# Low parts of eight value products made later, from unrounded copies, in a two-layer graph kernel

## The reference

```
h = relu(layernorm(x))
q, k, v = h @ Wq + bq, h @ Wk + bk, h @ Wv + bv
adj[src, dst] = 1
a = q @ k.T / sqrt(512);  a = a * adj + (1 - adj) * (-1e6)
x = x + softmax(a) @ v

h = relu(layernorm(x))
h = agg(h @ W1 + b1)            # normalised sum over edges and self loops
h = relu(gamma * (h - mean) / sqrt(var + 1e-5) + beta)     # over nodes
x = x + agg(h @ W2 + b2)
```

## Time and profile before

| | before |
|---|---|
| median of 3 runs | 307.56 us |
| profiled execution | 307.52 us |
| its traced span | 305.7 us |
| TensorE busy | 294.6 us (96%) |
| VectorE busy | 207.3 us (68%) |
| ScalarE busy | 160.0 us (52%) |
| GpSimd busy | 58.3 us (19%) |

### The profile page before, as it was taken

The page is one execution under the profiler, slowest core; times in us unless marked ns, Lnnn a source line. Parts: engine busy times, 40 slices in busy tenths (PEclk is TensorE's granted clock), DMA queues, the critical chain, the costliest instruction groups (busy, mean ns, idle before and its releaser), DMA issues.

```text
span 305.7 us, 4839 instructions
## 1 busy us (share of the span) xinstructions
PE 294.6 (96%) x1339; PEld 227.2 (74%) x1345; DVE 207.3 (68%) x458; ACT 160.0 (52%) x266; POOL 58.3 (19%) x103
## 2 busy tenths in 40 slices
PE   7999889899998999999999999999999999999995
PEld 6777346466665888888888888887888888878884
DVE  3889999999978557865758575568344388276311
ACT  3999967989546646545444454357523044342000
POOL 5352344000000530032131420203010044100000
PEclk9999999999999999999999999999999999999999
DMA  7816040000500309444362625323102000000221
GB/s 261 306 31 179 1 140 0 1 0 2 207 0 3 69 3 233 82 96 81 93 142 47 140 51 104 64 41 69 34 20 51 0 3 0 0 2 0 110 99 69
DMA packets 42312, 21.67 MB, mean 71 GB/s; under 512 B 35760, under 2 KB 36016, under 8 KB 42288
## 3 DMA queue, kind: packets, MB, share of 16 engines
q1 hardware_dynamic: 41744, 20.33, 26.3%
q10 hardware_dynamic: 544, 1.05, 1.0%
HBM read 10.88 MB, written 2.10 MB: 42 GB/s over the span
## 4 chain that ended last, share of the span: by engine, by line
PE 83%; DVE 8%; issue 3%; ACT 2%; DVEq 2%; DMA 1%; ACTq 0%
PE ps L986 19%; PE ps L988 19%; PE ps L987 18%; PE ps L1239 10%; PE ps L1162 8%; PE ps L1052 8%; DVE src_oh L705 1%; DMA qk_raw<-L_gnn_Wk_in 1%; DVE WT L688 1%; DVE M L688 1%; DVEq L705 1%; DVE wB L673 1%; DVE dst_oh L707 1%; PE ps L1020 1%; ACT lead_oh L473 0%
## 5 line engine op out<-in xcount | busy, mean ns | idle before, releaser
L705 DVE TENSOR_SCALAR src_oh<-iota,ecol 128x512 f16 x135 | 40.1, 352 | 5.0 <-issue 3.0
L1052 PE MATMUL ps<-src_oh,dst_oh 128*128 x131 | 33.3, 382 | 4.3 <-DVE dst_oh L707 3.1
L1162 PE MATMUL ps<-cnt,qh 128*128 128x512 f32 x128 | 30.1, 391 | 0.3 <-ACT cnt L575 0.3
L1052 PEld LDWEIGHTS ps<-src_oh,dst_oh 128*128 x135 | 13.3, 103 | 22.2 <-issue 12.8
L1239 PE MATMUL ps<-qh,cnt 128*128 128x512 f32 x128 | 29.3, 390 | 0.0
L1162 PEld LDWEIGHTS ps<-cnt,qh 128*128 128x128 f32 x128 | 23.9, 188 | 5.6 <-DVE qh L865 0.7
L1239 PEld LDWEIGHTS ps<-qh,cnt 128*128 128x128 f32 x128 | 23.9, 188 | 5.3 <-DVE vb L967 0.3
L988 PE MATMUL ps<-v,pT 128*128 128x512 f32 x64 | 25.0, 390 | 0.0
L986 PE MATMUL ps<-hT,qh 128*128 128x512 f32 x64 | 24.9, 389 | 0.0
L986 PE MATMUL ps<-v,pT 128*128 128x512 f32 x64 | 24.9, 389 | 0.0
L987 PE MATMUL ps<-v,pT 128*128 128x512 f32 x64 | 24.9, 389 | 0.0
(11 more groups left out here) (186 smaller groups left out, 685.2 us busy)
## 6 DMA issues: line engine op xcount, KB each, us to landing
xt<-x_in SPq DMA_DIRECT2D x16, 256.0 KB, 3.3
out<-xt SPq DMA_DIRECT2D x8, 256.0 KB, 2.1
qk_raw<-L_gnn_Wk_in ACTq DMA_DIRECT2D x2, 512.0 KB, 4.9
qk_raw<-L_gnn_Wq_in SPq DMA_DIRECT2D x2, 512.0 KB, 6.7
wB_raw<-L_gnn_Wv_in SPq DMA_DIRECT2D x2, 512.0 KB, 9.0
wB_raw<-L_gnn_W_in SPq DMA_DIRECT2D x2, 512.0 KB, 4.1
w_raw<-L_gnn_W_in SPq DMA_DIRECT2D x2, 512.0 KB, 4.3
bias_row<-L_gnn_b_in SPq DMA_DIRECT2D x2, 256.0 KB, 4.6
```

The lines of the kernel that those rows point to most:

```text
L705: dve.tensor_scalar(src_oh[:, bass.ds(slot, 1), j, :].rearrange("p a n -> p (a n)"), iota[:, :], ecol[:, bass.ds(c + j, 1)], None, ALU.is_ ...
L1052: m = pe.matmul(ps[:, i % 2, :], dst_oh[:, bass.ds(slot, 1), :, j].rearrange("p a n -> p (a n)"), lead_oh[:, i % 2, j, :] if first and ACT ...
L1162: m = pe.matmul(bank(g), qh[:, d, a, c * P:(c + 1) * P], cnt[:, d, n * HALF:(n + 1) * HALF], start=(d == 0 and a == 1), stop=last)
```

## The change

Each `v` item gets a second ScalarE activation, which copies the unrounded values from PSUM to `v_raw`, a tensor that lies on the place of `v` (the low part's own place). Its PSUM bank is then free (new semaphore `v_raw`). VectorE no longer makes low parts of `v` among the one-hots. It makes six of them, SBUF to SBUF, after the low part of `q` (1, 0), right ahead of the mask of block 0, and two after `large_flag`, ahead of the low part of the probabilities of block 0. They raise the new semaphore `v_lo`. GpSimd's first `add_bv` waits for six of them, and the first `weighted_v` for all eight. `item_lo` now counts without the `v` items, so that its waits use `nth_lo`.

```diff
-    v, zT, edge_i, edge_f, chunk1, hit, reach = shared(
-        [("v", [P, NT, 2, D], F32R)], [("zT", [P, 2, KC, N], F32R)],
+    v, v_raw, zT, edge_i, edge_f, chunk1, hit, reach = shared(
+        [("v", [P, NT, 2, D], F32R)], [("v_raw", [P, NT, 2, D], F32)], [("zT", [P, 2, KC, N], F32R)],
...
     items = list(start) + sum(ahead, []) + list(final)
     nth = lambda item: items.index(item) + 1
+    split_items = [item for item in items if item[0] != "v"]
+    nth_lo = lambda item: split_items.index(item) + 1
     item_bank = lambda item: start.get(item, final.get(item, 2 + (items.index(item) - len(start)) % ITEM_BANKS))
-    last_in = lambda b, end: max([n for n, other in enumerate(items[:end], 1) if item_bank(other) == b] + [0])
+
+    def left_bank(b, end):
+        before = [other for other in items[:end] if item_bank(other) == b]
+        if not before:
+            return None
+        if before[-1][0] == "v":
+            return S["v_raw"], before[-1][1] + 1
+        return S["item_lo"], nth_lo(before[-1])
+
 
     drel = lambda i: (drel_first if i < NW // 2 else drel_second)[:, i % (NW // 2), :]
...
+        pool.wait_ge(S["v_lo"], 6)
         for t in range(XT):
             add_bv(t)
...
             else:
                 act.activation(item_dest(item, 0), item_ps(item), ACT.Copy).then_inc(S["item_hi"], 1)
+            if what == "v":
+                act.activation(v_raw[:, n, 1, :], item_ps(item), ACT.Copy).then_inc(S["v_raw"], 1)
 
...
         def lo_of(item):
 
             what, n, c = item
+            if what == "v":
+                return
             dve.wait_ge(S["item_hi"], nth(item))
             hi = item_dest(item, 0).bitcast(F32)
             if what == "w":
...
                                          op1=ALU.subtract).then_inc(S["item_lo"], 1)
             else:
                 dve.tensor_tensor(item_dest(item, 1), item_ps(item), hi, ALU.subtract).then_inc(S["item_lo"], 1)
+
+        def v_lo(blocks):
+            for n in blocks:
+                dve.wait_ge(S["item_hi"], nth(("v", n, 0)))
+                dve.wait_ge(S["v_raw"], n + 1)
+                dve.tensor_tensor(v[:, n, 1, :], v_raw[:, n, 1, :], v[:, n, 0, :].bitcast(F32),
+                                  ALU.subtract).then_inc(S["v_lo"], 1)
 
         made = dve.alloc_register("made")
         dve.reg_mov(made, 0)
...
         lo_of(("q", 1, 0))
+        v_lo(range(0, 6))
...
             if i == 0:
                 large_flag()
+                v_lo(range(6, NT))
                 p16_lo(0)
...
-            if last_in(item_bank(item), i - 1):
-                pe.wait_ge(S["item_lo"], last_in(item_bank(item), i - 1))
+            left = left_bank(item_bank(item), i - 1)
+            if left:
+                pe.wait_ge(*left)
...
         def weighted_v(t):
             pe.wait_ge(S["p_hi"], t + 1)
             pe.wait_ge(S["p_lo"], t + 1)
+            if t == 0:
+                pe.wait_ge(S["v_lo"], NT)
             if t >= 1:
```

More of the change, by code:

```diff
@@ L164, in gnn_kernel @@
     Wk_in0 Wk_in1 Wq_in0 Wq_in1 wB_in0 wB_in1 w2_in0 w2_in1 w_hi w_lo
-    x_sums x_means x_squares ln_scale ln_coef h_ready item_ps item_hi item_lo uw_ready hw_second fill_ready
+    x_sums x_means x_squares ln_scale ln_coef h_ready item_ps item_hi item_lo v_raw v_lo uw_ready hw_second fill_ready
     ncol_ready lead_cols lead_dist lead_made onehots onehots_used c_done c16 loops_added adj_in0 adj_in1 adj_in2 adj_in3
@@ L744, in mask_level @@
                 dve.wait_ge(S["uw_ready"], 4)
-                dve.wait_ge(S["item_lo"], nth(("w", 0, 0)))
+                dve.wait_ge(S["item_lo"], nth_lo(("w", 0, 0)))
             else:
@@ L1023, in make @@
             if what == "m":
-                pe.wait_ge(S["item_lo"], nth(("t", Q, n)))
+                pe.wait_ge(S["item_lo"], nth_lo(("t", Q, n)))
             else:
-                pe.wait_ge(S["item_lo"], nth(("h", n if what == "v" else 4 * n + 3, 0)))
+                pe.wait_ge(S["item_lo"], nth_lo(("h", n if what == "v" else 4 * n + 3, 0)))
             if item == ("v", 0, 0):
@@ L1104, in scores @@
                 pe.wait_ge(S["c16"], 2 * NW)
-                pe.wait_ge(S["item_lo"], nth(("q", 0, KC - 1)))
+                pe.wait_ge(S["item_lo"], nth_lo(("q", 0, KC - 1)))
             if t == 4:
-                pe.wait_ge(S["item_lo"], len(items))
+                pe.wait_ge(S["item_lo"], len(split_items))
             if t >= 2:
@@ L1170, in _ @@
                 pe.wait_ge(S["degm_ready"], 1)
-                pe.wait_ge(S["item_lo"], last_in(6, nth(("q", 1, 0))))
+                pe.wait_ge(*left_bank(6, nth(("q", 1, 0))))
                 pe.transpose(bank(6)[:, 0:P], degm[:, 0:1].to_broadcast([P, P]), ident[:, :]).then_inc(S["degm_ps"], 1)
```

## The result

The kernel before took 308.34 us (median of 6 runs, 307.32 to 308.64), the changed one 310.75 us (6 runs, 309.92 to 311.38). The ratio is 1.0084, with a 95% interval of 1.0066 to 1.0103: 2.6 us slower, 2.0 to 3.2. The two medians are 2.41 us apart. Two later executions, at 496 us of the kernel before and 763 us of experiment 8, were in a slower state, and no ratio counts them.

What follows compares the result with a forecast made beforehand. TensorE was taken as the bound, following ScalarE's leads rather than VectorE in the stage of the counts. Terms 0 + 0.49 + 1.0 + 0 + 0 gave +1.5 us, so 309.0 us, range 307.3 to 310.1.

Steps and rivals of the forecast that it cites:

- VectorE's eight subtractions: Removed from the one-hots between 48 and 81 us: 4.8 us of work hidden beside TensorE, gain taken as 0.
- rival C: TensorE follows VectorE among the one-hots, so relieving it makes the kernel faster: -1.1 us, 306.4; chance 0.12.
- `v` 3: ScalarE's copy at 52.52 us delays the leads of window 5, and TensorE with them: +0.49 us.
- `v` 0 to 2: ScalarE's copies at 35.6 to 46 us, with leads over 2 us early and pauses behind them: 0.
- `v` 7: ScalarE's copy at 77.36 us, ahead of a 1.24 us wait for the closed counts: 0.
- `v` 4 to 6: Three ScalarE copies from 63.40 to 72.69 us, 1.47 us until the leads of window 9: +1.0 us.
- 0.35 of stall: TensorE's wait for late leads of window 9, possible between 0 and 0.65 us, taken as 0.35.
- 0.65 of stock: TensorE's loss around window 9 from having no instructions issued ahead, 0.78 us at full, taken as 0.65.
- Six subtractions before the mask: On VectorE behind `q` (1, 0): 3.6 us inside an idle of 4.06, 0.45 left, mask not later: 0.
- Two subtractions ahead of `p_lo`: On VectorE ahead of the probabilities' low part: 1.2 us in a pause of 1.79, 0.6 left: 0.
- rival A: VectorE blocked behind GpSimd's sums at shared ports, making TensorE late at 122 us: +0.6 us, 309.6; chance 0.16.
- GpSimd's sums: Four sums moved to start at about 108.3 us and end near 113.3, first reader at 128: 0 by itself.

Runs made afterwards that it cites:

- experiment 8: Changed kernel, ScalarE's leads first, two subtractions behind windows 11 and 13, six before the mask, GpSimd waiting for all eight: 307.94 us, ratio 0.9981.
- Experiment 4: Kernel before without the eight low parts of `v`, TensorE reading the high part instead: 307.67 against 307.70 us, ratio 0.9999.
- experiment 7: Kernel before with eight tiny VectorE memsets of an unused tile ahead of the second layer's branches: 308.20 against 307.82 us, ratio 1.0008.
- Experiment 3: Changed kernel without GpSimd's wait for six low parts, its sums running beside the six subtractions: 315.44 us, ratio 1.0255 to the kernel before.
- experiment 1: Changed kernel with copies of `v` 3 to 7 moved behind the counts of windows 5 and 9 to 12: 309.05 us, ratio 1.0032 to kernel before.
- experiment 2: Kernel before with ScalarE's additional `v` copies alone, VectorE keeping its subtractions: 310.42 against 307.70 us, ratio 1.0082.
- experiment 5: Kernel before with ScalarE making the next window's leads ahead of the items' high parts: 307.49 against 307.82 us, ratio 0.9976.
- experiment 6: Changed kernel with ScalarE making the next window's leads ahead of high parts and copies: 307.50 us, ratio 0.9984 to the kernel before.
- experiment 10: As experiment 8, plus the last `q` low part behind window 15's one-hots and eight tiny VectorE memsets: 307.05 us, ratio 0.9972 to kernel before.

## Why the prediction was right and wrong

Slower was right, and so was the main reason: the copies delay ScalarE's leads and VectorE's relief brings nothing. The size was wrong: +1.5 forecast, +2.6 measured (2.41 between the medians), and 310.75 lies above the range's 310.1. Of the 1.75 us between 309.0 and 310.75, 0.9 is this size, and 0.8 is that the kernel before itself came out at 308.34 with six runs instead of 307.56 with three, of which two had the short start-up. From 307.56 the same change would have ended at 310.0 to 310.2, at the range's upper edge. Point by point:

- VectorE's eight subtractions, 0: right. Experiment 4 measures it at -0.03 us, and rival C is gone with it.
- `v` 3, +0.49: right to the digit (0.66 became 1.15), since the forecast took the spacing of 0.49 straight from a row. `v` 0 to 2 and `v` 7, 0: right.
- `v` 4 to 6, +1.0 out of 0.35 of stall and 0.65 of stock: **mis-sized and wrongly split.** Measured +1.29, all stock and no stall, and in windows 7, 8 and 9, 0.4 to 0.5 each. I had the loss come at window 9 when ScalarE's slack of 0.64 was used up. But there was no slack between the leads and TensorE: I had written myself that stock thins once the leads come about 1.3 us ahead, and in windows 7 and 8 of the kernel before, which I didn't look at, they already came 1.21 and 1.43 ahead. From there each copy ahead of the leads costs nearly the whole of its 0.49, three times. So the 0.35 of stall was a term for a wait that never came, and the 0.65 of stock was half of what stock cost.
- Six subtractions before the mask, 3.6 us and 0.45 left: right (3.69 and 0.46).
- Two subtractions ahead of `p_lo`, 0: **wrong,** +0.41. This is rival A, which I gave 0.16 with 0.6 us: VectorE was held up beside GpSimd's sums by 0.59 us at the small sum and 0.55 at the two subtractions. I took it that nothing showed VectorE as the engine that waits, and let an unseen cost count as none, at a place where I had found no slack at all behind it.
- The second layer, not named: **missed,** +0.42. Added instructions moved a pause of VectorE far behind the change (experiment 7).
- GpSimd's sums start 0.08 us after the sixth subtraction and harm no reader: right. Experiment 3 shows that without the wait the change would have cost three times as much.

All three errors have the same sign, and two lie at places that the sum held at 0, so the range ended too low. That the four steps add up to 2.61 us in one pair of profiles and the ratio gives 2.6 is partly luck, with 2.0 to 3.2 as its interval.

## What to carry to other kernels

When two helpers are full, relieve the one whose result the main engine takes last; the other's relief was worth nothing here, however full it was. A helper's result can set the main engine's pace without a wait in the profile: compare the time from its end to the next work in several windows, and where it is constant there is no slack. On that helper make the awaited result first and the copies second: the order was worth 3.1 us in the changed kernel and 0.7 in the old one (2.9 and 1.1 by the traces), with no work removed. Price a two-input operation from SBUF on VectorE by what runs on GpSimd in the same microseconds, and look for slack behind it before calling it free.

## What the runs showed of the hardware

- TensorE can lose 0.4 to 0.5 us per window without waiting for anything that the profile names, once its input comes 0.7 to 1.0 us ahead instead of 1.2 to 1.4. The second group of chunks behind it came 2.3 to 2.6 us after the end of the input in windows 5, 7, 8 and 9 of both kernels and of experiments 1 to 4 and 7. That the pace follows the leads is shown by this and by experiments 1, 5 and 6; that a stock of issued instructions is what ties them is argued.
- After 3.91 us of waiting in experiment 3 the granted clock fell to a mean of 0.60 for 4 us, which cost another 1.6 us; behind the idle times of 0.6 and 1.2 us that TensorE has in the changed kernel the granted clock stays at 1.00.
- VectorE's pause after its first statistics is 0.24 or 0.61 us by what stands ahead in its program (experiment 7), and it can move to the operation before (experiment 10).
- The start-up has two forms. The first eight transposes at 5 us take 0.86 us in some executions and 1.57 in others, in variants of either kernel, while the granted clock reads 1.00 in both, and all that follows is 0.9 to 1.4 us later. Why is open. The times of the kernel before fall into two groups to match, most of them near 307.4 and near 308.6. Two rows, of the changed kernel and of before:

```profile
4.98 1.57 PEld L1045 LDWEIGHTS ps<-ident,qk_raw 128*128 128x128 f32 x8 [0.50 <-DMA qk_raw<-L_gnn_Wk_in]
```

```profile
5.10 0.86 PEld L1020 LDWEIGHTS ps<-ident,qk_raw 128*128 128x128 f32 x8 [0.61 <-DMA qk_raw<-L_gnn_Wk_in]
```

A profile of one form set against a profile of the other shows a microsecond that is no one's doing; I took it off before I compared.
